# Fourteen routed groups of the expert stage run among the calls of the last four batches

## The reference

```python
x = L0_attn_x                                            # (16, 512, 256)
x = layernorm(x + causal_attention(x))                   # q, k of 16 channels, values are x itself
x = layernorm(x + x @ (ternary(W) * scale).T)
x = layernorm(x + L1_attn(x))                            # q/k statistics, a small "ODE" along the sequence, channel gate, projection
# the last half layer, on all 8192 tokens:
h = layernorm(x) * gamma + beta
shared_out = silu(h @ sw1.T) @ sw2.T                     # 256 -> 512 -> 256
probs = softmax(h @ router_w.T)                          # 8 experts
top_prob, top_idx = max(probs), argmax(probs)
routed_out = top_prob * (silu(h @ ew1[top_idx].T) @ ew2[top_idx].T)
x = layernorm(x + shared_out + routed_out)
```

## Time and profile before

| | us |
|---|---|
| three timed runs: median (lowest to highest) | 820.53 (819.62 to 824.59) |
| the profiled execution, its own time | 819.63 |
| its span, first to last instruction | 818.3 |
| PE busy in the span | 730.1 (89%), mean clock 0.965 |
| DVE busy | 705.3 (86%) |
| ACT busy | 656.3 (80%) |
| POOL busy | 340.0 (42%) |
| first gTr of the group stage starts | 620.54 |

### The profile page before, as it was taken

How to read it: one execution, slowest core, us unless ns; L and a number is a source line. 1 busy time by engine, 2 the same in 40 slices (tenths; PEclk the granted TensorE clock), 3 DMA queues, 4 the chain that set the end, 5 groups by cost and what they waited for, 6 DMA issues and landing times.

```text
span 818.3 us, 18493 instructions
## 1 busy us (share of the span) xinstructions
PE 730.1 (89%) x5412; PEld 547.7 (67%) x5412; DVE 705.3 (86%) x2105; ACT 656.3 (80%) x1445; POOL 340.0 (42%) x370
## 2 busy tenths in 40 slices
PE   3769998999999999999999999998567999888872
PEld 2556676687777767767777776775335777767761
DVE  5768888899999989999999999988766999988885
ACT  2366669988997997997898799787563999999994
POOL 3000011133524334333353342536363498777667
PEclk9979999999999999999999999999687999999997
DMA  7113201212223132240222220102025367755430
GB/s 261 30 49 88 97 27 52 83 30 79 78 85 98 53 104 79 64 119 27 80 91 85 85 85 27 65 28 78 33 72 165 113 194 224 199 163 154 149 120 29
DMA packets 57217, 76.51 MB, mean 93 GB/s; under 512 B 15453, under 2 KB 37919, under 8 KB 57120
## 3 DMA queue, kind: packets, MB, share of 16 engines
q1 hardware_dynamic: 46016, 48.45, 20.8%
q0 software_dynamic: 9600, 25.25, 8.6%
q10 hardware_dynamic: 1504, 1.64, 0.6%
HBM read 47.42 MB, written 28.91 MB: 93 GB/s over the span
## 4 chain that ended last, share of the span: by engine, by line
PE 58%; issue 12%; ACT 9%; DVE 8%; POOL 8%; DMA 2%; ACTq 1%; SPq 1%; DVEq 0%; POOLq 0%
PE bank L618 8%; PE bank L839 6%; PE bank L826 4%; ACT G_S L1961 4%; PE bank L567 4%; POOL out L3748 4%; PE bank L699 3%; PE bank L701 3%; PE bank L700 3%; PE bank L711 3%; PE bank L796 2%; PE bank L646 2%; PE bank L630 2%; ACT G_y L1977 2%; PE bank L647 2%
## 5 line engine op out<-in xcount | busy, mean ns | idle before, releaser
L3562 POOL TENSOR_TENSOR R<-rstd,mhalf 128x4 f32<-128x4 f32 x16 | 19.2, 1200 | 265.3 <-DVE rstd L2018 265.3
L3748 POOL DMA_INDIRECT out<-G_y,Gid x72 | 83.3, 1157 | 39.4 <-ACT G_y L1977 17.2
L1961 ACT ACTIVATE G_S<-bank,e1b,e1s 128x256 f32<-128x256 f32 (+1 forms) x188 | 88.1, 582 | 4.1 <-PE bank L1376 4.1
L1376 PE MATMUL bank<-G_T,E1T 128*128 128x256 f16 (+1 forms) x752 | 77.2, 254 | 8.0 <-issue 6.4
L618 PE MATMUL bank<-X,PT 128*128 128x257 f32 x320 | 83.8, 402 | 0.4 <-ACT PT L1419 0.4
L3606 POOL DMA_INDIRECT rrec<-R,pos x64 | 67.3, 1052 | 29.5 <-issue 22.5
L3597 POOL DMA_INDIRECT hrec<-HN,pos x64 | 65.4, 1022 | 27.0 <-issue 15.7
L1376 PEld LDWEIGHTS bank<-G_T,E1T 128*128 x752 | 60.9, 100 | 19.3 <-issue 12.0
L1388 PE MATMUL bank<-E2T,G_Sh 128*128 x288 | 66.1, 276 | 8.5 <-DVE G_Sl L3537 8.2
L618 PEld LDWEIGHTS bank<-X,PT 128*128 128x128 f32 x320 | 60.2, 200 | 10.5 <-issue 1.4
L839 PE MATMUL bank<-E2T,Sh 128*128 128x256 f16 x256 | 60.4, 281 | 6.8 <-DVE Sl L2198 6.7
(11 more groups left out here) (414 smaller groups left out, 2355.9 us busy)
## 6 DMA issues: line engine op xcount, KB each, us to landing
XT<-in_xT SPq DMA_DIRECT2D x16, 512.0 KB, 4.0
X<-in_x SPq DMA_DIRECT2D x16, 512.0 KB, 5.8
G_h<-hrec SPq DMA_DIRECT2D x25, 257.0 KB
G_r<-rrec SPq DMA_DIRECT2D x25, 257.0 KB, 3.5
e1n<-in_ew SPq DMA_DIRECT2D x8, 512.0 KB, 3.5
e2n<-in_ew SPq DMA_DIRECT2D x8, 512.0 KB, 3.4
G_h<-hrec SPq DMA_DIRECT2D x22, 128.5 KB
G_r<-rrec SPq DMA_DIRECT2D x22, 128.5 KB, 2.5
```

Source lines behind the costliest of these rows:

```text
L1376: last = pe.matmul(bk[:, o + a:o + b], E1T[:, e, c, ff * P:(ff + 1) * P], gt[:, x, c, a:b], start=k == 0, stop=k == 3)
L1961: last = act.activation(G_S[w % NGS][:, ff, a:b], bk[:, o + a:o + b], ACT.Silu, bias=e1b[:, e, ff], scale=e1s[:, e, ff])
L3748: pool.indirect_dma_start(t["out"], bass.IndirectOffsetOnAxis(Gid[w % NGI][:, j:j + 1], 0), G_y[w % NGY][:, j, :], None, bounds_check=TOK ...
```

## The change

The tokens of the first BEARLY = 12 batches are counted when batch 12 is ranked. From these counts ten new DVE steps, early(0) to early(9), make a first list of NEARLY = 14 full groups (12 batches hold at least that many). The order of calls from the last four batches on is written anew in all four lists: these groups, and the first steps of groups 14 to 17, stand among the calls of batches 12 to 15. The loops over w start at WLOOP = 18 and are otherwise as before. rank(15) counts all tokens; sort(), now eleven steps, lists only the other NLATE = 11 full groups, in a table of runs that counts what the first list has taken from each expert; mix() has a third run per expert (NRUN = 24). counts() is gone. Buffers move so that the first groups' tiles are free by then: G_Sh and G_Sl lie over X2 tiles and late U tiles. Groups below NSINGLE = 11 (and every even one) use bank 0 for their transposes and bank 2 for down; odd ones from 11 on banks 6 and 7, which the batches use until their end.

```diff
-NRUN = 2 * NE
+NRUN = 3 * NE
+BEARLY = 12
+NEARLY = 14
+NSINGLE = 11
+WLOOP = 18
+NLATE = NF - NEARLY
...
+    def tr_bank(w):
+        return banks[0 if w < NSINGLE or w % 2 == 0 else 6]
+    def down_bank(w):
+        return banks[2 if w < NSINGLE or w % 2 == 0 else 7]
+    def before_in_bank(w):
+        if w < NSINGLE or w % 2 == 0:
+            return w - 1 if w <= NSINGLE else w - 2
+        return w - 2 if w - 2 >= NSINGLE else -1
...
             if w == 0:
+                sp.wait_ge(s["early"], NFIRST)
+                sp.wait_ge(s["zero"], 32 * NGT)
+                sp.wait_ge(s["hrec0"], 8 * NT * BEARLY)
+                sp.wait_ge(s["hrec1"], 8 * NT * BEARLY)
+                sp.wait_ge(s["x2"], at("x2", B - 1, 1))
+                sp.wait_ge(s["x3"], at("x3", B - 3, NT - 1))
+            if w == NEARLY:
                 sp.wait_ge(s["sort"], NSORT)
-                sp.wait_ge(s["zero"], 32 * NGT)
                 sp.wait_ge(s["hrec0"], 8 * NT * B)
                 sp.wait_ge(s["hrec1"], 8 * NT * B)
...
         row_of = {}
-        for w in range(NG + 7):
-            gload(w - 3)
-            pads(w - 1)
-            rload(w - 7)
+        for w in range(NEARLY):
+            gload(w)
+            if w < NGR:
+                rload(w)
+            elif w > NGR:
+                rload(w - 1)
+        rload(NEARLY - 1)
+        for w in range(NEARLY, NG + 4):
+            gload(w)
...
+            if b == BEARLY:
+                pe.matmul(total, onesb[:], ACC[b % 2][:], start=True, stop=True)
+            if b == B - 1:
+                pe.matmul(total, onesb[:], ACC[b % 2][:], start=True, stop=False)
+                for j in range(NT):
+                    pe.matmul(total, onesb[:], tile(j), start=False, stop=j == NT - 1)
...
+        def gTr(w):
...
+            pe.wait_ge(s[f"gath{w % NGR}"], gathered(w))
+            if before_in_bank(w) >= 0:
+                pe.wait_ge(s["gTl"], at("gTl", before_in_bank(w)))
...
+            if j == 0:
+                if before_in_bank(w) >= 0:
+                    pe.wait_ge(s["gy"], at("gy", before_in_bank(w)))
+                elif w > 0:
+                    pe.wait_ge(s["y"], at("y", B - 1, 3))
+                else:
+                    pe.wait_ge(s["ode"], NO * (B // GB))
...
-        for w in range(NG + 7):
+        for w in range(WLOOP, NG + 7):
             gTr(w)
...
+        def early(k):
+            if k >= 1:
+                dve.wait_ge(s["early"], k)
+            if k == 0:
+                dve.wait_ge(s["rank"], at("rank", BEARLY))
+                dve.memset(q_z[:], 0.0)
+                dve.memset(r_dd[:], 0.0)
+                dve.tensor_copy(r_rs[:, 0:NE], expert_first[:])
+                ins = dve.tensor_copy(q1_ni[:], banks[6][:, NT * NE:(NT + 1) * NE])
...
+            elif k == 4:
+                dve.tensor_tensor(r_d[:, 0:2 * NE - 1], r_rs[:, 1:2 * NE], r_rs[:, 0:2 * NE - 1], ALU.subtract)
+                ins = dve.tensor_tensor(q1_ge[:], q1_end[:, :, None].to_broadcast([P, NE, NEARLY]), group_w[:, None, 0:NEARLY].to_broadcast([P, NE, NEARLY]), ALU.is_le)
+            elif k == 5:
+                dve.scalar_tensor_tensor(r_dd[:, 0:NE], r_cnt[:, 0:NE], -float(SLOT), r_d[:, 0:NE], ALU.mult, ALU.add)
+                ins = dve.tensor_reduce(q1_ex[:], q1_ge[:].rearrange("p e g -> p g e"), AX.X, ALU.add)
...
-                ins = dve.tensor_tensor(q_ge[:], q_end[:, :, None].to_broadcast([P, NE, NF]), group_w[:, None, :].to_broadcast([P, NE, NF]), ALU.is_le)
             elif k == 5:
+                ins = dve.tensor_tensor(q_ge[:], r_end[:, :, None].to_broadcast([P, 2 * NE, NLATE]), group_w[:, None, NEARLY:NF].to_broadcast([P, 2 * NE, NLATE]), ALU.is_le)
...
-    NCONST, NREST, NSORT, NMIX, NWSC = 7, 50, 10, 10, 17
+    NFIRST = 10
+    NCONST, NREST, NSORT, NMIX, NWSC = 7, 50, 11, 11, 17
```

More of the change, by code:

```diff
@@ L1303, in pe_program @@
         rank(13)
+        gTr(1)
         gn1(7)
@@ new lines, in dve_program @@
+        gTl(7)
+        sort(3)
+        gbn(3, 1)
+        Sl_(14, 0)
+        Sl_(14, 1)
+        gmv(3, 0)
+        gy(4)
+        gnb_(2)
+        gmv(3, 1)
+        gx(4)
+        gve(3)
+        rg(15)
+        sort(4)
+        Sl_(14, 2)
+        Sl_(14, 3)
+        gbn(4, 0)
+        gbn(4, 1)
+        gTl(8)
+        gmv(4, 0)
+        gmv(4, 1)
+        sort(5)
+        gve(4)
+        gSl(5)
+        y(14, 0)
+        gnb_(3)
+        for i in range(1, 4):
+            y(14, i)
+        gnb_(4)
@@ new lines, in dve_program @@
+        sort(10)
+        gTl(10)
+        gx(7)
+        gy(8)
+        gbn(7, 0)
+        gx(8)
+        gbn(7, 1)
+        gbn(8, 0)
+        gSl(9)
+        gmv(7, 0)
+        gmv(7, 1)
+        gTl(11)
+        gve(7)
+        gbn(8, 1)
+        mix(0)
+        gSl(10)
+        gmv(8, 0)
+        mix(1)
+        gmv(8, 1)
+        gnb_(7)
+        gy(9)
+        gve(8)
+        gTl(12)
+        mix(2)
+        gx(9)
+        gTl(13)
+        gnb_(8)
+        gy(10)
+        gbn(9, 0)
+        mix(3)
@@ L3543, in dve_program @@
+        gbn(9, 1)
+        gx(10)
+        gmv(9, 0)
+        gmv(9, 1)
+        mix(4)
+        gve(9)
+        gbn(10, 0)
+        mix(5)
+        gSl(11)
+        mix(6)
+        gnb_(9)
+        gbn(10, 1)
+        gmv(10, 0)
+        mix(7)
+        gmv(10, 1)
+        mix(8)
+        gve(10)
+        gy(11)
+        mix(9)
+        gTl(14)
+        gSl(12)
+        gx(11)
+        gTl(15)
+        gnb_(10)
+        mix(10)
+        for w in range(WLOOP, NG + 7):
             gbn(w - 7, 0)
@@ L3752, in pool_program @@
+        gid_(15)
+        for w in range(WLOOP, NG + 7):
             scatter(w - 6, 0)
```

1476 lines of the change are left out of this document (915 added, 561 removed).

## The result

| | before | changed |
|---|---|---|
| time, median of 4 runs (us) | 820.08 | 793.95 |
| lowest and highest (us) | 812.52, 824.59 | 791.48, 795.28 |
| profiled execution and its span (us) | 819.6, 818.3 | 795.28, 794.0 |

The ratio to the kernel before is 0.9694, with a 95% interval of 0.9656 to 0.9733: 26 us faster. Measured again on three chips the changed kernel came out at 0.9694, 0.9697 and 0.9702. (Five executions of this study, two of the kernel before and one each of f3_act_more, k0_changed and k3_dve_more, were in the chip's slow state and are left out of the ratios.) The prediction was 804.5 us with a range from 796 to 815.

The account below looks back on a forecast made before the run. DVE's load was taken to bound the stretch before w = 18, where latency left a hole: gain 24.5 - 3.0 - 5.8 = 15.7 us, 819.6 - 15.7 = 803.9, with the median's offset 804.8, stated as 804.5 us; range 796 to 815.

Parts of the forecast that it names:

- Where the gain arises: Loops are the same from w = 18, so the end moves as that point does; first changed DVE row at 521.99.
- DVE's load: DVE's busy time from 521.99 us to w = 18: 138.5 + 5.2 for added steps = 143.7 us.
- Idle that stays: DVE idle before w = 18: 3.0 us ahead of gTl(0), 5.8 us behind it at 95% busy.
- The bound on the gain: With no DVE idle at all, w = 18 would come 168.2 - 143.7 = 24.5 us earlier.
- ACT near 85%: Sign in the changed kernel: ACT's busy share between about 558 and 640 us, with DVE at 94 to 97%.
- Wait 1, gather 0: gload(0) needs early step 10; gather lands 549 to 552.5, PE's gTr(0) about 557; cover 4.5 us.
- Wait 2: Gather 1, behind rload(0) on SP, is issued at 558 to 561 and lands by 564; no cover, no cost.
- Wait 3: Groups 14 to 17 need the full sort; group 14 ready at 132, gTl(14) at 139 of DVE's 143.7; cover 7 us.
- Rival A: Hole moved, not filled: last batches' chains wait behind group calls, DVE at 85% after 558; 818.5 us; chance 0.15.
- B: First eleven groups share single banks; serial link gTr, gT, gTl at 11.5 us gives 834 us; chance 0.07.
- C: POOL becomes the bound from hsc(15, 0) to the loop; rows stretched another 15% give 810 us; chance 0.06.
- D: Early start fails: gather 0 lands 10 us late, PE stops 5 us at gTr(0); 809.5 us at least; chance 0.06.

Follow-up runs that it names:

- f3_act_more: Changed kernel with eight more copies of 128x512 on ACT (5.8 us), spread between gT(1) and gT(14): 0.9681, beside 0.9694 for the changed kernel.
- k0_changed: The changed kernel itself, measured again on another chip beside the runs with added DVE load: 0.9702 of the kernel before.
- k3_dve_more: Changed kernel with nine unused additions of 128x512 floats on DVE (6.1 us), spread between gTl(0) and mix(0), on another chip: 0.9698, beside 0.9702.
- g1: Changed kernel with 70 small dependent DVE additions at w = 18 to 24, one behind each call: 795.75 us, 0.9710, beside 793.1 us.
- g2: Changed kernel with 70 small dependent DVE additions at w = 18 to 24, ten in a row per iteration: 803.6 us, 0.9818, beside 793.1 us.
- h1_order: Changed kernel with DVE's gSl(12) and gTl(14) put ahead of gy(11) and of mix(7) to mix(10): 789.2 us, 0.9637.
- f1: Changed kernel with nine unused additions of 128x512 floats on DVE (6.1 us), spread between gTl(0) and mix(0): 0.9684, beside 0.9694.
- k2: Changed kernel with 48 small dependent DVE additions between gTl(0) and mix(0), in four blocks of twelve in a row: 0.9821, beside 0.9702.
- e3: Changed kernel with early(9), on which gather 0's issue waits, moved on DVE to just ahead of gTl(0), 10 us later: 0.9814.
- e1: Changed kernel with all group calls and mix taken out of the last batches, run by the loops from w = 0: 1.0181.
- e2: Changed kernel with only groups 0 to 6 among the last batches' calls, groups 7 to 35 run by the loops: 0.9807.

## Why the prediction was right in kind and wrong in size, by its own steps

- **Where the gain arises.** Right: between 522 and w = 18, nothing behind it (128.4 us to the end for 128.1). One name in the frame was wrong: the row at 521.99 is x3(12, 1) and (12, 2), and x3(13, 0) starts at 523.52. The calls up to it are the same in both kernels, so the sum does not change. Where this text measures from x3(13, 0), it is the true one, at 523.72 in the changed kernel.
- **DVE's load.** The step that failed. 138.5 + 5.2 = 143.7 us; measured 133.2, so the term was 10.5 us too large. The added rows were charged too high by 1.8 (3.4 for 5.2 us). The greater part is that busy time is no fixed quantity: before, chains of small steps ran with DVE empty around them, and each link counted its full 0.19 us. Mixed with independent work it costs 0.07 to 0.1. That a small operation costs three to four times less among others is shown by g1 and g2; that the 8.9 us more of overlap are this effect is read from the rows, not shown by a run.
- **Idle that stays.** 3.0 + 5.8 = 8.8 us; measured 10.4 (1.9 up to 558.2). Size right; place wrong. It was to be spread evenly. From 558 to 640 it is 4.3 of 81.8 us, and from 640 to 665.6 it is 4.3 of 25.6: waits for PE's down, for POOL's rstd and for no one that the profile names. h1_order has them too.
- **The bound on the gain, 24.5 us, and with it the lower end of the range, 796.** Wrong twice. It was no bound, since it was made from a load that was too large; and the step "DVE's load is the largest, so it sets the time" failed too. 6.1 us of load that was added in short pieces cost nothing that could be measured (f1, k3; f3 on ACT), four pauses of 2.4 us cost about their length (k2).
- **ACT near 85%.** Wrong: 78.95 of 81.80 us, 96.5%. The load was sized right (129.8 forecast, 128.3 measured over the whole stretch); I had not divided it: 31.4 us of it lie ahead of 558 and 17.9 behind 640. The two table loads are there, 32 in place of 30.
- **Clock and PE.** The clock is 0.98 from 558 to 640 (0.81 before, forecast 1.00), PE's load 129.7 us (130).
- **Wait 1, gather 0.** Right: q_offi at 547.4, issue at 548.6 (546 to 549), gTr(0) at 556.7 (557) with no wait. The price of losing the cover was right as far as PE's wait goes, 4.9 us in e3; what it costs at the end is open.
- **Wait 2.** Gather 1 was issued at 557.0 (558 to 561), no cost. **Wait 3.** gload(14) was issued at 649.5, 127.5 us behind 522 (127); gTl(14) ran at 662.1, 140.1 (139). Not DMA but DVE's own order made it late. Where the groups run late, in e1 and e2, the same gather did hold PE up.
- **Rival A** (the hole is moved): refuted from 558 to 640, with DVE at 94.8% (94 to 97 was forecast) and PE's waits for Sl down to 0.8 us from the 6.7 of the earlier trace rows. A small part of it is true behind 640. **B** (banks): not at eleven groups, about 7 us at seventeen. **C** (POOL): DVE waited for its rstd once, for 1.3 us, and POOL itself waited 10.8 us for ACT's G_y between 560 and 690; it did not bound. G_Sl took 1276 ns from 558 to 640 us (median), with POOL busy 56 of 82 us, and no more than the 1278 to 1350 of before, so POOL's work cost DVE nothing there. **D** (gather 0 late): did not happen.

The miss was no accident of one chip, as the ratio was the same in four measurements. In the terms of the sum the gain was 15.7 us + 10.5 of load - 1.6 of idle = 24.6. This adds up by its making, since busy and idle time make up the stretch; it tells which term was off, and not what sets the time. As f1 and k3 show that a few microseconds of load do not set it, what does is known only in part: the hand-overs, by k2 and by the reading above.

## What to carry to other kernels

Where work is moved into a hole, do not add busy times of the two sides as they stand: steps of a latency chain shrink when independent work surrounds them, here from about 0.2 to 0.07 us for each small operation. Take what an operation costs from start-to-start spacings in a dense stretch. An engine at 95% need not be the bound: try it with a few microseconds of dead load, the same load once in small pieces and once in blocks. If only the blocks cost, look for the place where one engine meets two ready operations behind a waiting one, and turn them round.
